# Vision tower with two attentions and routed experts: the order of the first attention on TensorE, and more and wider filling matmuls

## The reference, cut to what matters

```python
h = tok(x)                                     # 32 images, 25 patches of 16x16: 800 tokens of 192 channels
h = layernorm(h + attn0(h))                    # first attention, below
h = layernorm(h + moe(h))                      # 8 experts (192 -> 768 -> 192), the best two of each token
h = layernorm(h + attn1(h))                    # softmax(q0 k0) v - lam * softmax(q1 k1) v, 12 heads of 16
h = layernorm(h + attn2(h))                    # gated low-rank q, k, v; softmax attention, 12 heads of 16

def attn0(x):                                  # 8 heads of 24 channels, in two groups a of four heads h
    q  = (x @ Wq)                              # one query for each group: 2 x 24
    kv = (x @ Wkv)                             # keys and values of all 8 heads
    attn = softmax(k^T v * SCALE)              # 24 x 24 for each image and head: keys by values
    return (q @ attn) @ Wproj + bproj          # all heads of a group read the same query
```

## Time and profile before

| | us |
|---|---|
| median of 3 runs (lowest, highest) | 361.54 (361.49, 362.68) |
| profiled execution, its own time | 360.7 |
| its span in the profile | 358.9 |
| TensorE busy, instructions | 320.6 (89%), 3092 |
| VectorE busy | 163.5 (46%) |
| ScalarE busy | 88.3 (25%) |
| granted clock of TensorE, mean | 0.935 |

### The profile page before, as it was taken

The page is one execution under the profiler, slowest core; times in us unless marked ns, Lnnn a source line. Parts: engine busy times, 40 slices in busy tenths (PEclk is TensorE's granted clock), DMA queues, the critical chain, the costliest instruction groups (busy, mean ns, idle before and its releaser), DMA issues.

```text
span 358.9 us, 7355 instructions
## 1 busy us (share of the span) xinstructions
PE 320.6 (89%) x3092; PEld 262.5 (73%) x3092; DVE 163.5 (46%) x459; ACT 88.3 (25%) x204; POOL 70.8 (20%) x82
## 2 busy tenths in 40 slices
PE   5999857997799989999999999888999889889992
PEld 4875446885489989999999879754677758446771
DVE  0021357466611111111111077779987552766555
ACT  1021214423012221122111003742332121723230
POOL 8000000056223374433332231000001100000002
PEclk9999955598989999999999899998999999989996
DMA  7999200020016988999991220000000000000002
GB/s 281 336 290 299 67 4 3 2 69 2 11 44 194 299 293 247 285 287 304 303 296 58 79 80 2 0 2 2 5 2 0 3 0 2 0 2 3 2 0 69
DMA packets 11930, 37.91 MB, mean 106 GB/s; under 512 B 1783, under 2 KB 5751, under 8 KB 11666
## 3 DMA queue, kind: packets, MB, share of 16 engines
q1 hardware_dynamic: 9978, 33.52, 29.6%
q0 software_dynamic: 1920, 3.93, 3.6%
HBM read 34.25 MB, written 3.19 MB: 104 GB/s over the span
## 4 chain that ended last, share of the span: by engine, by line
PE 72%; DVE 17%; DMA 3%; issue 3%; ACT 3%; POOL 2%; POOLq 0%; DVEq 0%
PE ps L717 10%; PE ps L705 7%; PE ps L706 7%; PE ps L503 7%; PE ps L533 5%; PE ps L796 4%; PE ps L757 3%; PE ps L749 3%; PE ps L590 2%; PE ps L774 2%; DMA xs<-x_rows,from_row 2%; PE ps L550 2%; PE ps L784 2%; PE ps L577 2%; PE ps L551 2%
## 5 line engine op out<-in xcount | busy, mean ns | idle before, releaser
L435 POOL TENSOR_TENSOR rstd<-veps,neg_half 128x2 f32<-128x2 f32 (+1 forms) x16 | 10.6, 660 | 209.6 <-DVE veps L1151 209.6
L705 PE MATMUL ps<-xga,w1t 128*128 128x128 f32 x240 | 47.4, 279 | 0.0
L706 PE MATMUL ps<-xgb,w1u 65*128 65x128 f32 x240 | 47.4, 279 | 0.0
L1256 DVE COPY ys<-ps 128x192 f32<-128x192 f32 x20 | 7.2, 358 | 77.4 <-PE ps L717 77.4
L717 PE MATMUL ps<-w1t,hid 128*128 128x192 f32 x240 | 42.2, 326 | 0.0
L503 PE MATMUL ps<-w1a,consts 128*128 128x384 f32 x96 | 39.2, 540 | 0.0
L717 PEld LDWEIGHTS ps<-w1t,hid 128*128 128x128 f32 x240 | 38.6, 190 | 0.0
L982 ACT ACTIVATE hid<-ps 128x768 f32<-128x768 f32 x20 | 16.2, 810 | 87.2 <-PE ps L706 87.2
L705 PEld LDWEIGHTS ps<-xga,w1t 128*128 128x128 f32 x240 | 37.3, 195 | 0.1
L706 PEld LDWEIGHTS ps<-xgb,w1u 65*128 65x128 f32 x240 | 37.3, 195 | 0.0
L465 POOL DMA_INDIRECT y_rows<-ys,to_row x20 | 19.8, 988 | 57.4 <-DVE ys L1256 57.1
(11 more groups left out here) (223 smaller groups left out, 538.8 us busy)
## 6 DMA issues: line engine op xcount, KB each, us to landing
w1t<-in_wt SPq DMA_DIRECT2D x20, 960.0 KB, 5.6
w1u<-in_wu SPq DMA_DIRECT2D x20, 240.0 KB, 7.5
pat<-in_pat SPq DMA_DIRECT2D x6, 496.0 KB, 7.0
w1a<-in_w1a SPq DMA_DIRECT2D x1, 1322.0 KB
y<-y_rows SPq DMA_DIRECT2D x6, 192.0 KB, 3.4
w1b<-in_w1b SPq DMA_DIRECT2D x1, 835.2 KB
x_rows<-x_tok SPq DMA_DIRECT2D x3, 192.0 KB, 2.0
out<-x_tok SPq DMA_DIRECT2D x6, 96.0 KB, 1.7
```

Of the source, the lines that this page charges most:

```text
L705: pe.matmul(out, w1t[:, b, 128 * k:128 * k + 128], xga[:, j % 2, :], start=True, stop=False)
L706: mm = pe.matmul(out, w1u[0:CB + 1, b, 128 * k:128 * k + 128], xgb[:, j % 2, :], start=False, stop=True)
```

## The change

The first attention gets another order. On TensorE the queries come first, then kv of groups 0 to 4, then rounds 0 and 1 of the small products, then kv of groups 5 to 7. A round now takes four groups and two of the four images of each, and writes two banks: 0 and 1 in even rounds, 2 and 3 in odd ones, so that it waits for the shift of the round before the last. ScalarE copies kv of groups 0, 2, 4, 5, 6 and 7, VectorE of 1 and 3. The residual of the first attention is added by TensorE (`residual0`, an identity matmul for each tile), and VectorE's layernorm reads the sum in PSUM.

The filling changes: 3 to 6 matmuls in the gating (384 columns), 4 to 7 before the first gathered block (384), 4 new ones (384) ahead of the wait for the rows in the combination, 128 to 384 columns in each `keep_busy` of `to_channels` (two matmuls a pair), 4 new ones (384) at the start of each `attention`, ahead of the wait for queries and keys.

```diff
-                        keep_busy(spare[t // 2], 2)
+                        keep_busy(spare[t // 2], 2, 384)
...
+            def keys_values(g):
+                if 2 <= g < 4:
+                    pe.wait_ge(q0_act, 1)
+                    pe.wait_ge(q0_dve, 1)
+                if g in (4, 6):
+                    pe.wait_ge(kv_act, g // 2 - 1)
+                if g in (5, 7):
+                    pe.wait_ge(kv_dve, g // 2 - 1)
...
             def keys_by_values(r):
 
-                wait(pe, s0_shifted, r)
-                for gg in range(2):
-                    g = 2 * r + gg
+                pe.wait_ge(kv_act, 6 if r >= 2 else 2)
+                pe.wait_ge(kv_dve, 2)
+                wait(pe, s0_shifted, r - 1)
+                for g4 in range(4):
+                    g = 4 * (r // 2) + g4
                     for a in range(2):
...
-                            for i in range(IG):
...
+                            for i in range(2):
...
+            def residual0(ts):
+                for t in ts:
+                    n = rows(t)
+                    pe.matmul(proj0(t), ident[0:n, 0:n], x_tok[0:n, t, :], start=(t % 2 == 0), stop=False, skip_group_check=True)
...
+            queries()
+            for g in range(5):
+                keys_values(g)
+            keys_by_values(0)
+            keys_by_values(1)
+            for g in range(5, G):
+                keys_values(g)
+            turn_a0(0)
+            keys_by_values(2)
+            keep_busy(4, 6)
+            keys_by_values(3)
+            turn_a0(1)
+            by_queries(0)
+            by_queries(1)
+            pe.wait_ge(s0_shifted, 3)
+            residual0(range(0, 4))
+            turn_a0(2)
+            by_queries(2)
+            turn_a0(3)
+            for t in range(0, 3):
+                project0(t)
+            residual0(range(4, TT))
+            by_queries(3)
+            for t in range(3, TT):
+                project0(t)
...
-            keep_busy(3, 3, 384)
+            keep_busy(3, 6, 384)
...
-            keep_busy(3, 4, 384)
+            keep_busy(3, 7, 384)
...
+            keep_busy(4, 4, 384)
             pe.wait_ge(diag_done, PICKS)
...
+                pe.wait_ge(v_act, call + 1)
+                pe.wait_ge(v_dve, call + 1)
+                keep_busy(4, 4, 384)
                 pe.wait_ge(qk_act, QK_JOBS[call])
                 pe.wait_ge(qk_dve, QK_JOBS[call])
-                pe.wait_ge(v_act, call + 1)
-                pe.wait_ge(v_dve, call + 1)
...
-                if layer == 1:
+                if layer == 0:
+                    dve.wait_ge(proj_ready, t1)
+                elif layer == 1:
                     dve.wait_ge(h_ready, t1)
```

More of the change, by code:

```diff
@@ L543, in _ @@
             pe.wait_ge(pool_set, PREP)
-            for g in range(G):
-                half = 1 if GT * (g + 1) <= 512 else 2
-                pe.wait_ge(xa_done, half)
-                pe.wait_ge(xb_done, half)
-                if g >= 4:
-                    pe.wait_ge([kv_act, kv_dve][g % 2], (g - 4) // 2 + 1)
-                pe.matmul(ps[:, g % 4, 0:KV], padded(xpa, g), wkv0a[:, :], start=True, stop=False)
-                pe.matmul(ps[:, g % 4, 0:KV], padded(xpb[0:CB + 1], g), wkv0b[:, :], start=False, stop=True).then_inc(kv_ready, 1)
@@ L553, in _, with queries @@
-            for n in range(2):
-                out = ps[:, 4 + n, 0:HALF]
-                pe.matmul(out, wq0a, half_of(xpa, n), start=True, stop=False)
-                pe.matmul(out, wq0b, half_of(xpb[0:CB + 1], n), start=False, stop=True).then_inc(q0_ready, 1)
+            def queries():
+                pe.wait_ge(xa_done, 2)
+                pe.wait_ge(xb_done, 2)
+                for n in range(2):
+                    out = ps[:, 6 + n, 0:HALF]
+                    pe.matmul(out, wq0a, half_of(xpa, n), start=True, stop=False)
+                    pe.matmul(out, wq0b, half_of(xpb[0:CB + 1], n), start=False, stop=True).then_inc(q0_ready, 1)
@@ new lines, in keys_values @@
+            def keys_values(g):
[6 more added lines that the diff above has]
+                    pe.wait_ge(kv_dve, g // 2 - 1)
+                out = ps[:, 4 + g % 4, 0:KV]
+                pe.matmul(out, padded(xpa, g), wkv0a[:, :], start=True, stop=False)
+                pe.matmul(out, padded(xpb[0:CB + 1], g), wkv0b[:, :], start=False, stop=True).then_inc(kv_ready, 1)
@@ L581, in by_queries @@
+                for g4 in range(4):
+                    mm = pe.transpose(ps[:, 6 + r % 2, 128 * g4:128 * g4 + 128], a0[:, r % 2, g4, :, :, :], ident)
+                mm.then_inc(a0T_ready, 1)
             def by_queries(r):
                 pe.wait_ge(a0T_done, r + 1)
-                if r == 0:
-                    pe.wait_ge(q0_act, 1)
-                    pe.wait_ge(q0_dve, 1)
-                if r == 2:
+                if r < 2:
+                    pe.wait_ge(kv_act, 3 + r)
+                else:
@@ L588, in by_queries @@
                     pe.wait_ge(s0_shifted, 4)
-                for j in range(4):
-                    mm = pe.matmul(ps[:, O0_BANK[r // 2] + r % 2, 4 * N * j:4 * N * j + 4 * N], a0T[:, 4 * r + j, :],
-                                   q0[:, :, :, 4 * r + j, :].rearrange("p a b t -> p (a b) t"), start=True, stop=True)
+                for g4 in range(4):
+                    pair = 2 * (4 * (r // 2) + g4) + r % 2
+                    mm = pe.matmul(view(ps[:, O0_BANK[r], 2 * N * g4:2 * N * g4 + 1], [[256, 2], [N, 2], [1, N]]), a0T[:, 4 * r + g4, :],
+                                   q0[:, :, :, pair, :], start=True, stop=True)
@@ L614, in _, with project0 @@
+            def project0(t):
+                half = 1 if 128 * t + rows(t) <= HALF else 2
+                pe.wait_ge(o0_act, half)
+                pe.wait_ge(o0_dve, half)
                 n = rows(t)
                 for s in range(2):
-                    mm = pe.matmul(tok_bank(2, t), view(o0[:, 256 * t + s:256 * t + s + 1], [[2, n]]), wp0[:, s, :], start=(s == 0 and t % 2 == 0), stop=(s == 1), skip_group_check=True)
+                    mm = pe.matmul(proj0(t), view(o0[:, 256 * t + s:256 * t + s + 1], [[2, n]]), wp0[:, s, :], start=False, stop=(s == 1), skip_group_check=True)
```

174 lines of the change are left out of this document (80 added, 94 removed).

## The result

| | median, us | runs | lowest to highest |
|---|---|---|---|
| kernel before | 361.51 | 4 | 360.44 to 362.68 |
| changed kernel | 377.53 | 4 | 372.87 to 379.31 |

The ratio is 1.0399, with a 95% interval of 1.0297 to 1.0502: 4.0% slower. The forecast was 367.4 us in a range of 361.5 to 370.0. The sign was right, the time was 10 us too low and outside the range.

What follows compares the result with a forecast made beforehand. It saw TensorE as 89% busy, held up by waits, instruction supply and clock falls. Terms -0.5 + 0.1 - 1.7 + 2.5 + 2.6 + 2.5 + 2.0 - 1.6 = +5.9 took 361.5 to 367.4 us; range 361.5 to 370.

Steps and rivals of the forecast that it cites:

- The start of the first attention: Queries 2.8 us and five kv groups 7.6 us come first; small products start at 37.2 us instead of 41.44.
- the stop after 104 small products: Round 1 of the small products runs into the instruction supply at 39.2 us; TensorE idles 2.2 us.
- the chain of ScalarE copies ahead of the first projection: First projection waits for ScalarE's `o0` and `a0T` copies until 62.1 us; TensorE idle from 60.0 to 62.2.
- both `to_channels`: Wide filling in the two later transpositions to channels outlasts the waits: +2.6 and +2.5 us, low end 0 each.
- the third attention: Filling fits the 2.63 us wait ahead of the scores and avoids the clock fall behind it: -1.6 us.
- The second attention: Filling of 2.6 us ahead of the scores delays them and VectorE's first shift: +2.0 us.
- The rule on transposes: Transposes don't count as busy to the clock gate, so `to_channels` could lose the clock; no gain summed, rival 364.0, chance 0.04.
- I therefore take one fall here, and as its length the 3.5 us: First attention, rounds 0 and 1: one clock fall of 3.5 us, making three kv groups take 6.3 us instead of 4.5.
- so the earlier small products are all given back by this order: First attention: second `reorder` ends at 70.8 us against 69.96 before, despite the earlier start; whole term -0.5 us.
- that rival (371.4 us): Slower than forecast: first attention stays at half clock behind its third round, +4 us more; chance 0.11.
- The queue behind the first projection: Round 3's product by queries stands behind three projections and three residuals: 3.9 us with itself, plus 1.7 for the clock.
- -1.7 ahead of the experts: Three more matmuls before the first gathered block remove a 3.5 us half clock: -1.7 us, 0 if it falls anyway.

Runs made afterwards that it cites:

- the first attention alone: Kernel before with only the new first attention, every filling as before: 367.49 us, ratio 1.0143.

## Why the prediction missed

**What held.** The start of the first attention to within 0.2 us, the stop after 104 small products (1.89 us, forecast 2.2 after 103), the chain of ScalarE copies ahead of the first projection (2.09 us, forecast 2.2), both `to_channels` (+2.7 and +2.3 for +2.6 and +2.5) and the third attention (-1.5 in the trace, -1.4 by the ratio). The second attention was right in the trace (+1.8 for +2.0), not by the ratios (+4.8, from two sets of runs). The rule on transposes of the Trainium skill, TensorE: Matmul & The Clock Gate, section Part 4: PE-mode transpose, changed nothing here: both `to_channels` had a clock of 1.00 with the narrow filling and have 1.00 with the wide one. Whether transposes without any filling would lose the clock, no run here shows.

**The step that failed** is in the first attention: "I therefore take one fall here, and as its length the 3.5 us", and with it "so the earlier small products are all given back by this order", at a term of -0.5. Measured it is +4.9 in the profile and +5.2 by the ratio of the first attention alone. Of the 5.4 us between forecast and profile, 3.8 are the length of this fall: the gating starts at 87.59 us behind a fall of 17.1 us and at 83.81 behind one of 3.4, with the same instructions up to there. The forecast had the half clock over the three kv groups alone; in the changed kernel it went on over rounds 2 and 3 and their transposes, to 60.0 us. The other 1.6 us lie behind it. In the first attention alone, with its short fall, the first projection starts at 62.88 us (forecast 62.2), the product of round 3 ends at 68.9 (67.8), the projections at 76.6 (74.8).
- The place of this fall was right. Its length is 3.4 us in three of the eight profiles with these instructions, 6.8 in three and 17 in two, so which one a run gets is luck as far as these runs show. The range gave a longer fall only half of its price, +4 behind the third round; that rival (371.4 us) was the nearest one, at a chance of 0.11.
- The queue behind the first projection was seen, and priced well: 2.2 us of wait (2.09 measured), 1.7 for the clock over the first projections (1.7: 3.90 for 2.23 us) and 1.2 over the others (1.5: 4.50 for 2.99). What the forecast didn't do is set the order against itself without the queue; it set it against the kernel before (70.8 for 69.96 us). The queue is worth some 8 us at a first fall of equal length (10.2 and 11.2 by medians), more than any term of the sum.

**The mis-sized terms behind it.** The half clock was taken to go where filling stands (-1.7 ahead of the experts, measured -0.5; gating +0.1, measured +1.9). It came all the same, over the filling, which then costs 5.57 us in place of 4.0. That is one of two outcomes, and both occur. The gating part is +0.3 in the four profiles with this filling and no half clock over it, +1.8 to +2.0 in the four with one; the part ahead of the experts is -1.9 to -2.0 in the two profiles without a half clock there, -0.4 to -0.5 in the others. In the combination the forecast's low end was a clock that doesn't fall; it fell later and for 6.8 us, over the four fillings (4.73 us for 2.6): +4.1 for +2.5. In five other profiles with this filling the fall there is 3.4 us long, and the way from the first block's second product to the product with the picked rows takes 2.7 to 3.5 us more than before. A fall in queries and keys, +1.5, wasn't in the sum.

**The range** took each clock fall once, at the place where the trace before had it. Its upper end had no room for falls at new places.

**What stays open**: what decides the length of the first fall, why the filling ahead of the second attention costs 4.8 us by the ratios and 1.8 in the trace, and what else spreads the executions. The clock alone doesn't: of the first attention alone, the execution of 363.64 us had a mean granted clock of 0.950 and that of 368.37 us one of 0.959.

## What to carry to other kernels

When a new order puts an instruction behind a wait that isn't its own, cost the order against the same order without that, not against the kernel before. Count the clock with the wait: 4.3 us of waits less were 7.4 us less between two profiles, since the work behind them had run at half clock. Filling matmuls on the path are paid in full, and at half clock they are paid double; of the places tried only the one with a measured wait of 2.63 us ahead of work that then ran at half clock gave anything, 1.4 us. A trace shows one execution: where falls of the clock set the time, compare medians of several runs before believing in the place of any one.

## What was not expected of the hardware

- Full filling doesn't keep the clock. In the changed kernel it is at 0.50 from 210.2 to 217.0 us, with TensorE busy 6.80 of 6.80 us, and it was busy 10.00 of 10.00 us from 200 to 210 too; the last of that is 7 products with `gatesT` (8 rows) from 206.4 and the first of those with `x_tok`.
- The same instructions had their first fall at 42.5 for 3.4 us, at 42.9 for 17.1 and at 40.4 for 17.0 us in three kernels that are alike up to there. In all eight profiles with these instructions it begins between 40.0 and 42.9 us; it is 3.4 us long in three, 6.8 in three and 17.0 or 17.1 in two.
- The clock can fall long before the place that one studies: five of the other profiles have half the clock for 3.4 or 6.8 us from 23.9 to 24.9 us on, two of them of kernels that are the kernel before up to the combination or to `to_channels`. The kernel before had it full at 23.9 to 30.7 us.
- TensorE stopped with nothing to wait for after 104 small products in a row (x208), after some 95 (x191) when 4 transposes and wide products stood ahead, and after some 32 (x63) behind a full round and 4 transposes; each time for 1.5 to 2.5 us. Wide products of 4.7 us between two rounds were enough to take the stop away.
